# Two attention layers: the causal mask added on VectorE instead of TensorE, score units cut anew, the maxima's transfer put ahead of the keys', and the selection products of a slot in two parts

## The chip, the cores and the metric

The kernel runs on one core of a Trainium2 chip. The metric is the device time of one execution in microseconds. Five engines of the core matter: TensorE (PE in the profile, with PEld for its weight loads), VectorE (DVE), ScalarE (ACT), GpSimd (POOL) and SyncE (SP), which here only issues DMAs. Each works through its own list of instructions in order; they wait for each other by semaphores.

## The reference, cut to what matters

The program is two transformer-like layers over 16 sequences of 512 tokens with 128 channels. Each layer has one attention stage that this change touches. The first (called mla) projects to latents and has a rotary part; the second (mha) is plain:

```python
scores = jnp.einsum('bqhd,bkhd->bhqk', qq, kk) * scale      # 16 heads of 8
scores = jnp.where(causal[None, None], scores, jnp.finfo(scores.dtype).min)
probs = jax.nn.softmax(scores, axis=-1)
y = jnp.einsum('bhqk,bkhd->bqhd', probs, v).reshape(B, S, H)
```

What has to be computed for a head is: the scores of 512 queries with the keys up to each query, the maximum of each row, exp(score less maximum), the sum over keys, and the weighted values.

## The kernel before, in words

The stages run one after the other: a convolution layer's stages, attention mla, a layer of experts (glu), attention mha, and a second layer of experts (moe). Both attentions are made by one function, `attention_stage` (line 789).

**Turns and slots.** One sequence is a turn. A turn has four slots, g = 0 to 3, one for each group of four heads. `walk` (line 874) runs the first turn without probabilities, then a loop of inner turns, then turns without a next sequence, and a last one that only finishes. Each engine has its own function `slots` and walks over units k = 0, 1, 2, ... of a slot. What stands at which k is set by small tables (lines 863 to 872).

**Scores for the maxima.** TensorE computes scores of a unit (`scores`, L1394) into one of three PSUM banks, with queries on the partitions: 11 units for a slot (`UNITS1`). One matmul more for each unit (L1398) adds the mask: an identity times a table of 0 and -1e30. VectorE reduces each unit to its negated row maximum (L1101). After the last unit of a slot GpSimd splits the maxima into a high and a low part (L1187, L1188). In the next slot, behind unit k = 4, TensorE transposes them (L1441) and multiplies the previous output by selection matrices (L1446, four products of 128 by 36), VectorE copies the transposed maxima into `mhl` (L1068), and SyncE sends `mhl` by DMA into two extra rows of `Qb` (L952).

**Scores less maxima, probabilities, values.** One slot later TensorE recomputes the scores transposed, with the maxima as two more rows of the product (L1406): 10 units of 512 columns for a slot, 16 matmuls. ScalarE takes exp (L1297), GpSimd zeroes what lies above the diagonal (L1216), and in the slot after that TensorE multiplies by the values (L1414, four heads side by side in the array), in two places of a slot.

**The next sequence's queries and keys.** During a turn the projections for the next one are computed: latents in slot 0 (mla alone), keys and queries in slot 1, values in slot 2. They are split in high and low parts (`kh`, `kl`, `qh`, `ql`; the low parts by VectorE, L1059). SyncE copies them to the rows of `Kb` (three DMAs of 256 KB, L925 and L926) and `Qb` (twelve DMAs of 64 KB, each from 32 partitions to 8, L933 and L936). The keys' DMAs wait for `kb_used`, which TensorE gives at the end of slot 1. At the start of a turn TensorE waits for all fifteen (`k_rows`, `q_rows`) and for the maxima sent last (`m_rows`). SyncE's own list for an inner turn is: maxima in slot 0; maxima in slot 1; keys, maxima, queries in slot 2; maxima in slot 3.

## Time and profile before

| what | us |
|---|---|
| median of 3 runs (3221.18 to 3238.54) | 3233.5 |
| the profiled execution | 3232.98 |
| its span | 3231.2 |
| attention mla: first score unit reduced to last | 555.4 to 1347.4 |
| attention mha: first score unit reduced to last | 1903.1 to 2647.9 |

The profile is of one execution; its page gives the busy time of each engine, slices of the span, groups of instructions by line, waits and DMAs. "Busy" for TensorE is modelled (matmuls overlap, each row's duration holds the time through the array), so spacing between the starts of rows says more than their durations. A row of a timeline gives start, duration (both us), engine, line, operation, out<-in, sizes, how many instructions are merged, and in brackets the idle time before them and what ended it. PEclk is the granted TensorE clock as a share of 2.4 GHz. Over the whole span PE is busy 81%, DVE 67%, ACT 44%, POOL 36%. Both attentions together are about half of the time.

### The profile page before, as it was taken

To read this page: it belongs to the slowest core of one execution; us is meant where nothing else is said; L and a number is where in the kernel's file an instruction comes from. 1 tells how busy PE (TensorE), PEld (TensorE's weight loads), DVE (VectorE), ACT (ScalarE), POOL (GpSimd) and SP (SyncE) were. 2 spreads that over 40 slices of the span, in tenths; PEclk is the share of its full clock that TensorE was granted. 3 is DMA by queue.
4 is the path that set the end of the run, shared out by engine and by line. 5 is a ranking of instruction groups with operands and counts; after the bars stand their busy time and mean duration, and the time that the engine had idled before them with its cause. 6 is when DMAs were issued, how large, how long until landed. Compare 5 with 4: busy or idle time off the path is not lost. (4 is left out here: it accounts for less than half of the span.)

```text
span 3231.2 us, 51537 instructions
## 1 busy us (share of the span) xinstructions
PE 2618.4 (81%) x17479; PEld 2011.4 (62%) x17479; DVE 2178.6 (67%) x5628; ACT 1414.6 (44%) x2412; POOL 1177.9 (36%) x2298
## 2 busy tenths in 40 slices
PE   1445873999999999948888759999999997698972
PEld 1423662777777777636666647777777766486861
DVE  5733773777777767448888846676767754677785
ACT  0001330455555555511111225666666652586861
POOL 3210110334434344322222113454455442773076
PEclk9997995899999999969999969999999995799996
DMA  2144001213223222031110032222122114697772
GB/s 29 32 134 127 23 13 30 41 29 44 42 29 47 37 34 41 15 104 50 49 49 32 3 43 33 31 40 36 25 40 40 26 17 165 231 296 225 250 218 73
DMA packets 198657, 228.02 MB, mean 71 GB/s; under 512 B 48621, under 2 KB 148814, under 8 KB 190478
## 3 DMA queue, kind: packets, MB, share of 16 engines
q1 hardware_dynamic: 188302, 207.69, 26.7%
q0 software_dynamic: 8192, 16.79, 1.6%
q10 hardware_dynamic: 2048, 2.10, 0.2%
q8 instruction: 60, 0.98, 0.1%
q14 instruction: 55, 0.45, 0.0%
HBM read 132.55 MB, written 58.10 MB: 59 GB/s over the span
## 5 line engine op out<-in xcount | busy, mean ns | idle before, releaser
L1394 PE MATMUL banks<-Kb,Qb 96*128 96x128 f32 (+3 forms) x2048 | 599.6, 348 | 58.6 <-issue 27.3
L1406 PE MATMUL banks<-Qb,Kb 98*128 98x512 f32 (+3 forms) x2048 | 602.7, 356 | 4.8 <-ACT mha_prob L1297 1.0
L1101 DVE TENSOR_REDUCE mha_nm<-banks 128x1 f32<-128x384 f32 (+3 forms) x704 | 421.5, 639 | 185.9 <-PE banks L1398 172.3
L1101 DVE TENSOR_REDUCE mla_nm<-banks 128x1 f32<-128x384 f32 (+3 forms) x704 | 419.9, 638 | 160.0 <-PE banks L1398 146.5
L1297 ACT ACTIVATE mla_prob<-banks 128x512 f32<-128x512 f32 x640 | 376.5, 598 | 311.6 <-PE banks L1406 303.2
L1394 PEld LDWEIGHTS banks<-Kb,Qb 96*128 96x128 f32 x2048 | 364.3, 195 | 216.5 <-issue 159.9
L1297 ACT ACTIVATE mha_prob<-banks 128x512 f32<-128x512 f32 x640 | 375.7, 598 | 273.7 <-PE banks L1406 260.8
L1216 POOL TENSOR_SCALAR_AFFINE_SELECT mla_prob<-mla_prob 128x256 f32<-128x256 f32 (+1 forms) x640 | 237.8, 379 | 405.3 <-PE banks L1394 379.7
L1406 PEld LDWEIGHTS banks<-Qb,Kb 98*128 98x128 f32 x2048 | 334.8, 193 | 47.1 <-issue 7.6
L1216 POOL TENSOR_SCALAR_AFFINE_SELECT mha_prob<-mha_prob 128x256 f32<-128x256 f32 (+1 forms) x640 | 225.6, 361 | 355.4 <-PE banks L1394 329.2
L1828 PE MATMUL banks<-glu_wd,glu_hid 128*128 128x128 f32 x1024 | 147.7, 288 | 74.3 <-DVE glu_hid L1707 74.1
L1828 PEld LDWEIGHTS banks<-glu_wd,glu_hid 128*128 128x128 f32 x1024 | 130.5, 196 | 117.6 <-DVE glu_hid L1707 113.8
L2174 DVE TENSOR_TENSOR moe_hl<-moe_h,moe_hh 128x512 fp32r<-128x512 f32 x212 | 146.4, 692 | 78.7 <-ACT moe_h L2278 65.7
L1788 ACT ACTIVATE glu_sg<-banks 128x512 f32<-128x512 f32 x128 | 76.4, 597 | 262.2 <-PE banks L1802 262.2
L2277 ACT ACTIVATE moe_hh<-banks,moe_bt 128x512 fp32r<-128x512 f32 x212 | 146.1, 689 | 87.7 <-PE banks L2291 72.3
L1398 PE MATMUL banks<-mla_mask,mla_identr 128*128 128x128 f32 (+2 forms) x704 | 183.8, 261 | 0.0
L2227 POOL DMA_INDIRECT moe_gb<-results,moe_back_slot x128 | 131.2, 1025 | 143.5 <-SPq L1988 105.6
L1398 PE MATMUL banks<-mha_mask,mha_identr 128*128 128x128 f32 (+2 forms) x704 | 181.5, 258 | 0.0
L1414 PE MATMUL banks<-mla_prob,mla_V 128*9 128x512 f32 (+3 forms) x2048 | 169.1, 450 | 0.3
L1414 PE MATMUL banks<-mha_prob,mha_V 128*9 128x512 f32 (+3 forms) x2048 | 167.4, 446 | 0.2
L2214 POOL DMA_INDIRECT slots<-X,moe_slot x128 | 126.5, 988 | 67.3 <-issue 38.7
L1398 PEld LDWEIGHTS banks<-mla_mask,mla_identr 128*128 128x128 f32 x704 | 139.2, 198 | 8.5
(434 smaller groups left out, 5392.1 us busy)
## 6 DMA issues: line engine op xcount, KB each, us to landing
moe_wt<-expert_rows SPq DMA_DIRECT2D x53, 1024.0 KB
conv_tz<-conv_kernel SPq DMA_DIRECT2D x16, 1024.0 KB, 6.8
moe_xg<-slots SPq DMA_DIRECT2D x53, 256.0 KB
results<-moe_yt SPq DMA_DIRECT2D x53, 256.0 KB
Kb<-mla_kh SPq DMA_DIRECT2D x32, 256.0 KB, 4.9
Qb<-mla_qh SPq DMA_DIRECT2D x128, 64.0 KB
Kb<-mha_kh SPq DMA_DIRECT2D x32, 256.0 KB, 5.6
Qb<-mha_qh SPq DMA_DIRECT2D x128, 64.0 KB
```

What stands on the lines that cost most here:

```text
L1101: dve.tensor_reduce(nm[:, g % 2, h:h + heads, j], ps[:, bank1(g, k), 0:heads * w].rearrange("p (h k) -> p h k", h=heads), axis=AX.X, op=AL ...
L1216: pool.affine_select(out=part, in_=part, compare_op=ALU.is_ge, fill=0.0, base=0, pattern=pattern, channel_multiplier=-1).then_inc(p_ready, 1)
L1297: act.activation(prob[:, g % 2, k, :], ps[:, S2 + k % 2, :], ACT.Exp, scale=HD ** -0.5).then_inc(s2_free, 1)
L1394: one = pe.matmul(ps[:, bank, x * w:(x + 1) * w], Qb[0:MROW, u, g, h + x, j * P:(j + 1) * P], Kb[0:MROW, u, g, 0:w], start=(x == 0), stop= ...
L1398: pe.matmul(ps[:, bank, 0:heads * w].rearrange("p (x w) -> p x w", x=heads)[:, :, w - P:w], identr[:, :], mask[:, 0:heads, :], start=False ...
L1406: last = pe.matmul(ps[:, S2 + k % 2, at:at + w], Kb[0:MROW + 2, u, grp, kb * P:(kb + 1) * P], Qb[0:MROW + 2, u, grp, h, kb * P:L], start=T ...
L1414: last = pe.matmul(ps[32 * hh:32 * hh + HD + 1, OB, kb * P:L], V[:, u, kb, grp * HG + hh, :], prob[:, par, unit, at:at + w], start=(kb == ...
L1828: last = pe.matmul(ps[:, OB + e % 2, b * P:(b + 1) * P], hid[:, e % 2, b * P:(b + 1) * P], wd[:, e, :], start=True, stop=True)
L2174: dve.tensor_tensor(hl[:, k, :], h[:, k, :], f32(hh[:, k, :]), ALU.subtract).then_inc(hid_ready, 1)
L2214: pool.indirect_dma_start(slots_d, bass.IndirectOffsetOnAxis(slot[:, q, a, t:t + 1], 0), X[:, first + j, b, :], None).then_inc(scattered[q ...
L2227: pool.indirect_dma_start(gb[:, j % 2, a, b, :], None, res_d[q], bass.IndirectOffsetOnAxis(back_slot[:, q, a, t:t + 1], 0)).then_inc(gathe ...
L2277: act.activation(hh[:, k, :], ps[:, FB + k, :], ACT.Gelu_apprx_tanh, bias=bias)
```

## The change

- **Mask.** The mask matmuls are gone. VectorE's reduction of a piece is now `tensor_tensor_reduce`: it reads the scores and a mask table in SBUF, adds, negates, takes the minimum, and writes the sum to a scrap tile `junk`; it compiles to two instructions, the main one and one that writes the result.
- **Units.** A slot has 12 score units for the maxima: four of one piece of 512, four of a piece of 384 and one of 128, four of one piece of 256 (`ROWS`). It has 11 units of scores less maxima, 11 matmuls: four of 512, four of 384, and three of 512 in which two or four heads share one matmul (`UNITS2`). The values follow in three places (k = 5, 8, 10), each waiting for its own units.
- **Selection.** The transposed maxima and the first two selection products come behind k = 2, the other two behind k = 3.
- **Low parts and the rotary sum** move from VectorE to GpSimd (`low_part`, `add_turned`), and get tiles of their own (`sines`, `tmpq`).
- **Places.** The output product moves from slot 1 to slot 0; mla's keys are at (1,0) and (1,6), its queries at (1,9) and (1,11); mha's queries move to slot 2; the values' projection moves to slot 3.
- **SyncE.** In slot 2 the maxima's DMA comes ahead of the keys and the queries; the queries' pieces go in another order.

```diff
-UNITS1 = [(0, 0, HG)] + [(1, h, 2) for h in (0, 2)] + [(j, h, 1) for j in (2, 3) for h in range(HG)]
+UNITS = 3 * HG
+ROWS = [[(3, 0, L)], [(2, 0, 3 * P), (0, 3 * P, P)], [(1, 0, 2 * P)]]
+UNITS2 = [(0, h, 1) for h in range(HG)] + [(1, h, 1) for h in range(HG)] + [(2, 0, 2), (2, 2, 2), (3, 0, 4)]
...
-        KEYS = dict(pe=0, turn=2, act=5, low=6) if latent else dict(pe=0, act=2, low=4)
-        QUERIES = dict(pe=6, turn=8, act=10, low=1) if latent else dict(pe=6, act=8, low=9)
-        VALUES = dict(pe=7, act=9)
-        DENSE = dict(pe=WIDE, act=WIDE, pe2=WIDE, dve=WIDE, add=(6, 8), stats=6)
+        GATHER, VALUES_AT, OUT, SPLIT = 2, {5: (0,), 8: (1,), 10: (2, 3)}, 11, 9
+        DENSE = dict(pe=(0, 3), dve=(0, 5), add=((0, 8), (0, 10)), stats=(0, 7))
+            KEYS = dict(pe=((1, 0), (1, 6)), turn=(1, 7), add=(1, 8), act=(1, 10), low=(2, 0))
+            QUERIES = dict(pe=((1, 9), (1, 11)), turn=(2, 0), add=(2, 2), act=(2, 3), low=(2, 5))
+            NEXT_XS = dict(stats=(2, 8), rms=(2, 11), scale=((3, 1), (3, 3)))
+            KEYS = dict(pe=((1, 0),), act=(1, 2), low=(1, 4))
+            QUERIES = dict(pe=((2, 1),), act=(2, 3), low=(2, 5))
+        VALUES = dict(pe=(3, 1), act=(3, 3))
...
                 def slots(n, u, turn, prep, proj, dense):
                     for g in range(NG):
+                        if has_maxima(turn, g):
+
+                            par, grp, to = (g + 1) % 2, (g + 3) % NG, u if g else 1 - u
+                            sp.wait_ge(ml_ready, c.next(ml_ready))
+                            sp.dma_start(f32(Qb[MROW:MROW + 2, to, grp, :, :]),
+                                         f32(mhl[:, par, :])).then_inc(m_rows[par], 16)
                         if g == 2 and turn != "last":
                             sp.wait_ge(kb_used, c.next(kb_used))
                             if proj:
                                 keys(1 - u)
-                        if has_maxima(turn, g):
-
-                            par, grp, to = (g + 1) % 2, (g + 3) % NG, u if g else 1 - u
-                            sp.wait_ge(ml_ready, c.next(ml_ready))
-                            sp.dma_start(f32(Qb[MROW:MROW + 2, to, grp, :, :]),
-                                         f32(mhl[:, par, :])).then_inc(m_rows[par], 16)
-                        if g == 2 and turn != "last" and proj:
-                            queries(1 - u)
+                                queries(1 - u)
...
+                def row_maxima(g, k):
+                    h = k % HG
+                    dve.wait_ge(s1_ready, c.next(s1_ready))
+                    for j, at, w in ROWS[k // HG]:
+                        last = dve.tensor_tensor_reduce(junk[:, k % 3, at:at + w], ps[:, bank1(k), at:at + w], mask[:, L - w:L], -1.0,
+                                                        BIG, ALU.add, ALU.min, nm[:, g % 2, h, j:j + 1])
+                    last.then_inc(s1_free, 1)
...
+                def add_turned(parts, full, whole, product):
+                    pool.wait_ge(parts, c.next(parts))
+                    pool.tensor_tensor(whole[:, :], whole[:, :], product[:, :], ALU.add).then_inc(full, 1)
+
+                def low_part(high, whole, hi, lo, split_done):
+                    pool.wait_ge(high, c.next(high))
+                    pool.tensor_tensor(lo[:, :], whole[:, :], f32(hi[:, :]), ALU.subtract).then_inc(split_done, 1)
...
-                    pe.matmul(ps[:, bank, 0:heads * w].rearrange("p (x w) -> p x w", x=heads)[:, :, w - P:w],
-                              identr[:, :], mask[:, 0:heads, :], start=False, stop=True,
-                              skip_group_check=True).then_inc(s1_ready, 1)
+                def scores(g, u, k):
+
+                    h = k % HG
+                    pe.wait_ge(s1_free, c.next(s1_free))
+                    for j, at, w in ROWS[k // HG]:
+                        last = pe.matmul(ps[:, bank1(k), at:at + w], Qb[0:MROW, u, g, h, j * P:(j + 1) * P],
+                                         Kb[0:MROW, u, g, 0:w], start=True, stop=True)
+                    last.then_inc(s1_ready, 1)
```

Three places of the lists of instructions follow, each before and then after the change. The first is TensorE in the later units of a slot of mla (L1394 and L1411 are scores for the maxima, L1406 and L1420 scores less maxima, L1398 the mask, L1414 and L1427 the values).

```order
L1394 MATMUL banks<-Kb,Qb 128x512
L1398 MATMUL banks<-mla_mask,mla_identr 128x128
L1406 MATMUL banks<-Qb,Kb 128x512
L1394 MATMUL banks<-Kb,Qb 128x512
L1398 MATMUL banks<-mla_mask,mla_identr 128x128
L1406 MATMUL banks<-Qb,Kb 128x128
L1406 MATMUL banks<-Qb,Kb 128x384
L1414 MATMUL banks<-mla_prob,mla_V 9x256 x4
```

```order
L1411 MATMUL banks<-Kb,Qb 128x384
L1411 MATMUL banks<-Kb,Qb 128x128
L1420 MATMUL banks<-Qb,Kb 128x384
L1411 MATMUL banks<-Kb,Qb 128x256
L1420 MATMUL banks<-Qb,Kb 128x512
L1427 MATMUL banks<-mla_prob,mla_V 9x384 x4
```

The mask matmul behind each unit is gone, and the narrow piece of 128 columns has moved from the scores less maxima to the scores for the maxima. The second place is SyncE from the maxima of slot 1 on in an inner turn of mla (`mla_mhl` are the maxima, `mla_kh` and `mla_kl` the keys, `mla_qh` and `mla_ql` the queries; "waits" names the semaphore).

```order
L925 DMA Kb<-mla_kh 32x4x512 [waits mla_k_split,mla_kb_used]
L925 DMA Kb<-mla_kh 32x4x512
L926 DMA Kb<-mla_kl 32x4x512
L952 DMA Qb<-mla_mhl 2x16x128 [waits mla_ml_ready]
L933 DMA Qb<-mla_qh 8x4x512 [waits mla_q_split]
L933 DMA Qb<-mla_qh 8x4x512 x7
L936 DMA Qb<-mla_ql 8x4x512 x4
L952 DMA Qb<-mla_mhl 2x16x128 [waits mla_ml_ready]
```

```order
L954 DMA Qb<-mla_mhl 2x16x128 [waits mla_ml_ready] x4
L935 DMA Kb<-mla_kh 32x4x512 [waits mla_k_split,mla_kb_used]
L935 DMA Kb<-mla_kl 32x4x512
L935 DMA Kb<-mla_kh 32x4x512
L942 DMA Qb<-mla_qh 8x4x512 [waits mla_q_split]
L942 DMA Qb<-mla_qh 8x4x512
L942 DMA Qb<-mla_ql 8x4x512
L942 DMA Qb<-mla_qh 8x4x512 x2
```

The maxima of slot 2 now stand ahead of the keys; nothing stands between keys and queries any more, and the maxima of slot 3 still stand behind the queries. The third place is VectorE in mla, around the rotary step of the keys in slot 1 (`sinr` and `cosr` are the tables of sines and cosines).

```order
L1101 TENSOR_REDUCE mla_nm<-banks 128x2 x2
L1052 TENSOR_TENSOR mla_xs<-banks,mla_sinr 128x512
L1053 TENSOR_TENSOR mla_tmp<-banks,mla_cosr 128x512
L1055 TENSOR_TENSOR mla_tmp<-mla_tmp,mla_xs 128x512
L1101 TENSOR_REDUCE mla_nm<-banks 128x1 x2
L1068 CAST mla_mhl<-banks 32x128
```

```order
L1093 ISA mla_junk,mla_nm<-banks,mla_mask 128x384
L1093 ISA mla_nm 128x1
L1093 ISA mla_junk,mla_nm<-banks,mla_mask 128x128
L1093 ISA mla_nm 128x1
L1056 TENSOR_TENSOR mla_sines<-banks,mla_sinr 128x512
L1057 TENSOR_TENSOR mla_tmp<-banks,mla_cosr 128x512
L1093 ISA mla_junk,mla_nm<-banks,mla_mask 128x256
```

One reduction of up to four heads has become a pair of instructions for every head and piece: 16 pairs for a slot where 11 reductions stood; and the sum of the two products (L1055) has left VectorE.

## Rows read from the trace of the kernel before

**Rows 1.** Busy time by stretch: a steady stretch of mla, one of mha.
```profile
core 0: us, PE busy (x) PEld busy (x) DVE busy (x) ACT busy (x) POOL busy (x), PEclk, DMA share, GB/s
800.00:1000.00 200.00, 194.53 (x1495) 146.05 (x1494) 154.42 (x315) 116.27 (x206) 85.54 (x223) 1.00 0.25 38
...
2200.00:2400.00 200.00, 196.52 (x1561) 149.90 (x1551) 140.04 (x287) 123.78 (x216) 97.34 (x249) 1.00 0.25 37
```
**Rows 2.** Timeline of TensorE: the first unit of slots and turns.
```profile
849.00 0.63 PE L1394 MATMUL banks<-Kb,Qb 96*128 96x128 f32 x4 [0.79 <-DVE mla_nm L1101]
...
875.36 0.63 PE L1394 MATMUL banks<-Kb,Qb 96*128 96x128 f32 x4 [0.29 <-issue]
...
948.26 0.64 PE L1394 MATMUL banks<-Kb,Qb 96*128 96x128 f32 x4 [0.79 <-DVE mla_nm L1101]
...
1987.80 0.63 PE L1394 MATMUL banks<-Kb,Qb 96*128 96x128 f32 x4 [0.37 <-DVE mha_nm L1101]
...
2011.75 0.63 PE L1394 MATMUL banks<-Kb,Qb 96*128 96x128 f32 x4 [0.26 <-DVE mha_nm L1101]
...
2130.07 0.63 PE L1394 MATMUL banks<-Kb,Qb 96*128 96x128 f32 x4 [0.30 <-DVE mha_nm L1101]
```
**Rows 3.** Timeline of TensorE, single units of mla.
```profile
856.55 0.22 PE L1398 MATMUL banks<-mla_mask,mla_identr 128*128 128x128 f32 x1
856.61 0.50 PE L1406 MATMUL banks<-Qb,Kb 98*128 98x128 f32 x2
856.95 0.40 PE L1339 MATMUL banks<-mla_xth,mla_lath 128*96 128x512 f32 x1
857.18 0.40 PE L1340 MATMUL banks<-mla_xth,mla_latl 128*96 128x512 f32 x1
```
**Rows 4.** Timeline of VectorE, mla.
```profile
850.66 2.81 DVE L1101 TENSOR_REDUCE mla_nm<-banks 128x4 f32<-128x512 f32 x5 [1.71 <-PE banks L1398]
...
883.05 0.38 DVE L108 BATCH_NORM_AGGREGATE mla_mv<-mla_st 128x2 f32<-128x6 f32 x4
...
883.83 0.16 DVE L1036 TENSOR_TENSOR mla_var<-mla_var,mla_mv 128x4 f32<-128x4 f32 x1
```
**Rows 5.** Timeline of SyncE: a turn of mha, then the same places in mla.
```profile
2011.57 1.24 SPq L925 DMA_DIRECT2D Kb<-mha_kh  x2
...
2016.81 0.66 SPq L952 DMA_DIRECT2D Qb<-mha_mhl  x1
2017.52 6.86 SPq L933 DMA_DIRECT2D Qb<-mha_qh  x8
...
881.78 0.67 SPq L952 DMA_DIRECT2D Qb<-mla_mhl  x1
```
**Rows 6.** Stretches of the same turn of mha: DMA share and GB/s.
```profile
2014.00:2018.40 4.40, 4.40 (x37) 2.91 (x36) 2.95 (x8) 1.92 (x4) 4.12 (x7) 1.00 1.03 122
...
2025.00:2031.20 6.20, 6.20 (x51) 4.49 (x49) 4.36 (x10) 3.55 (x8) 2.58 (x7) 1.00 0.52 62
2031.20:2032.20 1.00, 1.00 (x8) 0.88 (x7) 0.93 (x3) 1.00 (x2) 0.63 (x2) 1.00 0.12 11
```
**Rows 7.** mha's second turn starts: TensorE's row, then stretches around it.
```profile
1938.82 0.63 PE L1394 MATMUL banks<-Kb,Qb 96*128 96x128 f32 x4 [1.52 <-DMA Qb<-mha_mhl]
...
1937.70:1938.80 1.10, 0.00 (x0) 0.01 (x1) 0.34 (x1) 0.42 (x1) 0.42 (x2) 1.00 0.00 0
...
1940.90:1947.70 6.80, 6.80 (x35) 4.39 (x33) 2.66 (x7) 2.14 (x4) 1.01 (x3) 0.50 0.01 2
```
**Rows 8.** Stretches of the convolution stage, then of mla.
```profile
205.90:210.40 4.50, 0.13 (x8) 0.12 (x8) 0.69 (x1) 0.00 (x0) 0.40 (x1) 1.00 0.99 276
210.40:213.80 3.40, 3.40 (x24) 1.04 (x25) 0.00 (x0) 0.00 (x0) 0.00 (x0) 0.50 0.75 287
...
1122.00:1125.20 3.20, 2.39 (x14) 1.67 (x14) 3.05 (x6) 2.00 (x4) 1.34 (x3) 0.99 0.34 76
1125.20:1128.50 3.30, 3.30 (x14) 3.20 (x14) 3.02 (x6) 1.44 (x4) 2.53 (x6) 0.50 1.07 128
```

More of the change, by code:

```diff
@@ L943, in slots @@
                     for g in range(NG):
-                        if g == 2 and turn != "last":
-                            sp.wait_ge(kb_used, c.next(kb_used))
-                            if proj:
-                                keys(1 - u)
                         if has_maxima(turn, g):
@@ L1335, in _, with three @@
                 pe.sem_inc(s2_free, 2)
-                def three(o, hi, lo, a, first=True, last=True):
+                def three(o, hi, lo, first=True, last=True):
                     pe.matmul(o, hi, xth[:, :], start=first, stop=False)
@@ new lines, in new_values @@
+                def new_values():
+                    pe.wait_ge(ma_free, c.next(ma_free))
+                    for b in range(BLK):
+                        tok = slice(b * P, (b + 1) * P)
+                        o = ps[:, MA, tok]
+                        if latent:
+                            last = pe.matmul(o, lats[:, 1, tok], up[:, 3, :], start=True, stop=True)
+                        else:
+                            pe.matmul(o, xth[:, tok], wph[:, 1, :], start=True, stop=False)
+                            pe.matmul(o, xth[:, tok], wpl[:, 1, :], start=False, stop=False)
+                            last = pe.matmul(o, xtl[:, tok], wph[:, 1, :], start=False, stop=True)
+                    last.then_inc(v_ready, 1)
@@ L1502, in _ @@
                 pe.drain().then_inc(xs_taken, 1)
-                for g in range(NG):
-                    project(g, 0)
+                if latent:
+                    latents(1)
+                    latents(0)
+                for part in range(len(KEYS["pe"])):
+                    keys(part)
+                for part in range(len(QUERIES["pe"])):
+                    queries(part)
+                new_values()
                 transpose_x()
```

383 lines of the change are left out of this document (178 added, 205 removed).

## The prediction

> **What bounds the kernel now.** I read the busy times by stretch first. In both attentions TensorE is busy 97 to 98% of the time at the full granted clock (194.5 and 196.5 of 200 us), VectorE 77% and 70%, ScalarE about 60%, GpSimd 43% and 49% [rows 1]. So TensorE sets the pace inside a turn. Then the timeline of TensorE, for the rhythm: mla takes 99.26 us for two turns (849.00 to 948.26), 49.6 for one, of which slots 0 and 1 take 26.36; mha takes 142.27 for three (1987.80 to 2130.07), 47.4 for one, of which slots 0 and 1 take 23.95 [rows 2]. Last the timeline of SyncE and the stretches with DMA traffic, because TensorE may not start a turn before the keys, the queries and slot 3's maxima have landed. There the reader is to see a second chain that is only just hidden, as long as about half a turn. I think that this chain decides.
>
> **The chain of transfers.** In a turn of mha the first keys' DMA is issued at 2011.57 [rows 5]. From 2014 to 2018.4 the keys move at 122 GB/s with all DMA engines busy; then the queries move at 62 GB/s with half of them busy, with no pause, until the last maxima at about 2032 [rows 6]. That is 20.4 us from the first keys' issue to the last maxima, and in this turn keys and queries are back to back, as they will be after the change. From data there to TensorE going on it is another 1.2 us: in mha's second turn nothing moves from 1937.70 on, and TensorE starts at 1938.82, after 1.52 us of waiting for exactly this DMA [rows 7]. So a turn can't start earlier than 21.6 us after its keys' issue. Before, the keys are issued when slot 1 ends, which is why it fits in slots 2 and 3 (23.3 and 23.5 us, rows 2).
>
> **What the change does to TensorE.** Gone are 11 mask matmuls for a slot, 2048 columns. A 512 column matmul takes 0.23 us (856.95 to 857.18), a narrow mask matmul 0.06 (856.55 to 856.61), and a narrow one makes its neighbour late: 128 and 384 columns take 0.34 together [rows 3], 0.11 more than one of 512, which I put half on each. Masks: 2048 columns at 0.23 us for 512 is 0.92, and nine narrow ones at 0.05 is 0.45, so 1.37. Fewer, wider units of scores less maxima: four splits less, -0.2. A third break for the values and a second for the selection: +0.3, taken as three breaks at the 0.11 of the split; it lies between 0 and 0.5. Net -1.3 us for a slot, with 0.9 to 1.6 as its ends. Slots 0 and 1 of mla then take 26.36 - 2.6 = 23.8. In mha the queries leave slot 1 as well (three matmuls of 512, 0.7): 23.95 - 2.6 - 0.7 = 20.6. TensorE alone would need 49.6 - 5.2 = 44.4 for a turn of mla and 42.2 for one of mha.
>
> **VectorE.** Five reductions, three of 512 and two of 384, took 2.81 us [rows 4]: about 0.60 and 0.465 from start to start, so 0.33 for 256 and 0.20 for 128 columns. Before: 7 x 0.60 + 4 x 0.465 = 6.06 a slot. After: four heads x (0.60 + 0.465 + 0.33 + 0.20) = 6.38, plus 16 instructions that write a result. The trace has none of these. From below: four small aggregations in 0.38 us, 0.07 for each further one. From above: 0.16, the duration of a tiny operation, plus the 0.08 by which a reduction's duration (0.68) exceeds its spacing, if the second waits for the first: 0.24 [rows 4]. I take 0.07, since nothing between the two instructions waits on a semaphore: 16 x 0.07 = 1.1, so 7.5 a slot, +1.4. Four operations of 512 (0.6 to 0.9 us) leave for GpSimd in a turn of mla, two in mha: -0.75 and -0.4 a slot. VectorE goes from 9.6 to 10.2 us a slot in mla and from 8.3 to 9.3 in mha: below TensorE's 11.1 and 10.6, but in mla's slot 2, which gets the queries' rotary step beside the statistics, VectorE needs 11.4. GpSimd gets these operations; even at 2 us each they add 8 us to the 21 it is busy in a turn of mla. ScalarE gets one unit more a slot. Both are covered.
>
> The Trainium skill (VectorE: DVE Perf Modes, section "Two Vector instructions with no wait between them") says that an operation which also writes its accumulator is two instructions, each held back only by different start quadrants. All operands here start at partition 0. By that rule 0.07 is right; the trace of before can't show it.
>
> **What the change does to the chain.** The maxima of slot 2 now go first on SyncE, so the keys' DMA waits for them. They are issued 5.1 us after TensorE starts slot 2 in mha (2011.75 and 2016.81) and 6.4 us in mla (875.36 and 881.78) [rows 2, 5]. After: VectorE needs 4 x 0.67 + 0.8 = 3.5 us for units 0 to 4 instead of 2.7, in mla 1.2 more for the rotary step, but it comes into slot 2 less late, TensorE having more to spare of it: I take 4.9 us in mha and 5.9 in mla. One issue takes 0.7 (2016.81 to 2017.52). The new turn's start after the start of slot 2 is then
> - mla: 5.9 + 0.7 + 20.4 + 1.2 = 28.2 us, where slots 2 and 3 need about 22;
> - mha: 4.9 + 0.7 + 20.4 + 1.2 = 27.2 us, where they need 21.7.
>
> The queries' split isn't late for this: it stands behind unit 5 of 12, so about 6 us into slot 2, and takes GpSimd 2 us at most, while the keys occupy the queue for 6.7 us from their issue (2011.57 to 2018.3), until 12 us into the slot. So TensorE stands still for about 6 us at the end of each turn. Turn: mla 23.8 + 28.2 = 52.0, mha 20.6 + 27.2 = 47.8. Added work and the lost cover together eat all of what the masks give.
>
> **The clock.** 4.4 us of idle TensorE (205.9 to 210.4) was followed by 3.4 us at half the clock, 1.2 GHz, with TensorE busy; in mla a stretch with only 2.39 of 3.2 us busy was followed by half the clock too [rows 8], and the 1.5 us wait at 1938 by 6.8 us of it [rows 7]. After 6 us of idle I expect it at each turn's start, where TensorE is the bound: 3.4 us at half speed loses 1.7 us, 6.8 would lose 3.4. I take 1.7. Turn: mla 53.7, mha 49.5.
>
> **Sum.** 14 turns of each attention: 14 x (53.7 - 49.65) + 14 x (49.5 - 47.4) = 57 + 29 = 86. Before already has two stretches of 10 us at half clock in mla (one of them in rows 8), 9 us that are not lost twice: -9. First turns, which have no probabilities and so are short in slots 0 and 1: mha's grows from 37 to about 44 since the chain is as long there, mla's by 2: +9. Last turns have nothing to fetch: 4 x -1.3 each, -10. Sum +76. The profiled execution took 3232.98 us, 1.8 more than its span and within 0.02% of the median of 3233.5, so the sum stands for both: 3233 + 76 = 3309 us. The ends: 1.6 instead of 1.3 a slot and no clock loss, 3245; 0.9 and 3.4 us of clock loss, 3385.
>
> **Rivals.**
> - *The clock holds.* As above without the 1.7: 14 x (2.35 + 0.4) = 38, and +9 - 10, so 3270 with the 9 us kept. For it: a turn has one long pause only, and mla's turns mostly kept the clock.
> - *The result write is dear* (0.24). 16 x 0.17 = 2.7 us more VectorE a slot: 12.9 in mla, above TensorE in slots 0 and 1 by about 1 each, and 1 later at slot 2's maxima: some +3 in mla, +4 in mha with the finishing statistics in slot 0. 14 x 7 = 98: 3407. Against it: the small aggregations overlap.
> - *Faster: the queries spread over more DMA engines.* They move with a DMA share of 0.52 [rows 6]. The new order alternates rows of three parts of `Qb`. If the bound is the rows written to, they could go at the pace of issue, 0.71 us from start to start (2016.81 to 2017.52, rows 5): twelve take 8.5 us instead of the 12.8 from 2018.4 to 2031.2, the chain is 4.3 shorter: mla 49.4, mha 45.2 with the clock's loss. 14 x -2.45 = -34, less the 9 and 1: 3189. It decides once the chain of 20.4 is under 18. Against it: the last four DMAs of a turn already go to changing rows and gain nothing, the rate being 62 GB/s throughout [rows 6].
> - *Faster: the chain doesn't bind*, the slots do: mla 23.8 + 22 = 45.8, mha 42.2. 14 x -9.05 = -127, -18 for the rest (the 9 of the clock, and the first and last turns): about 3088. For it speaks only that I may misjudge when the keys can go; the list of SyncE says that they can't.
>
> The Trainium skill (DMA: Bandwidth & Descriptors, section "Why a DMA increments its semaphore by 16 and not by 1") says that a DMA from SyncE runs on as many engines, up to 16, as divide the slowest dimension on both sides: 8 for 32 partitions to 8. The share of 0.52 agrees; by that rule the order of the pieces changes nothing, and the third rival falls.
>
> **Chances.** Forecast 0.42; clock holds 0.15; dear write 0.10; spread queries 0.14; chain not binding 0.11; the last 0.08 for sums that cancel within the bound. No change, within 0.5% (16 us, about what a measurement of this kernel can tell): 0.10, of it 0.02 from the second case. Slower by more 0.65, faster by more 0.25. The likeliest case's own range is 3245 to 3385. The range reaches into the faster cases as far as the spread queries, and leaves out the unbound chain and the dearest write: 3175 to 3385.
>
> **What would show it.** On TensorE's first unit of a turn a wait of 4 to 7 us for the DMA of the maxima, turns 52 to 54 and 47.5 to 50 us long; keys issued 5.5 to 7 us into slot 2; half clock in the first microseconds of a turn; the pair on VectorE at 0.67 us for 512 columns. Wrong if turns start with no wait for a DMA, or if the keys' DMAs stand at the end of slot 1.

## The result, and the profile after

The changed kernel takes 3360.2 us (median of 4, 3348.7 to 3370.1) where the kernel before takes 3234.4: a ratio of 1.0395, 95% interval 1.0349 to 1.0441, 126 us more. The forecast was 76 more, 3309, in a range of 3175 to 3385. The profiled execution's span is 3347.0 us against 3231.2, 116 more; the two attention stages, from first to last instruction on their tiles, hold 114 of it: mla 953 us for 894, mha 895 for 839. One of run 8's four executions below took 4206.9 us, at a mean granted clock of 0.57 where the other three had 0.87, and is in no comparison.

First the waits of TensorE, whole kernel (line, what it waited for, us in total, times, longest):

```profile
PE banks L1411 <- DMA Qb<-mla_mhl: 72.8, 14, 5.8
PE banks L1411 <- DMA Qb<-mha_mhl: 70.7, 14, 5.5
```

There are 28 waits for the maxima's DMA, 5.1 us each: one at the start of every turn from the third on. The second turn, behind the short first one, waits 1.5 us in mla and 0.9 in mha. In the kernel before there is one such wait [rows 7]. Then the timeline around one turn of mla and one of mha, TensorE's rows:

```profile
813.56 0.76 PE L1411 MATMUL banks<-Kb,Qb 96*128 96x512 f32 x1 [5.78 <-DMA Qb<-mla_mhl]
...
842.03 0.47 PE L1411 MATMUL banks<-Kb,Qb 96*128 96x512 f32 x1 [0.26 <-DVE mla_nm L1093]
...
868.79 0.77 PE L1411 MATMUL banks<-Kb,Qb 96*128 96x512 f32 x1 [5.26 <-DMA Qb<-mla_mhl]
...
2286.93 0.47 PE L1411 MATMUL banks<-Kb,Qb 96*128 96x512 f32 x1 [0.26 <-issue]
...
2313.48 0.76 PE L1411 MATMUL banks<-Kb,Qb 96*128 96x512 f32 x1 [5.35 <-DMA Qb<-mha_mhl]
```

and SyncE's:

```profile
847.56 0.64 SPq L954 DMA_DIRECT2D Qb<-mla_mhl  x1
848.31 0.60 SPq L935 DMA_DIRECT2D Kb<-mla_kh  x1
...
2292.72 0.59 SPq L935 DMA_DIRECT2D Kb<-mha_kh  x1
```

Slot 2 of mla starts at 842.03, its maxima go at 847.56, the keys behind them at 848.31, and TensorE starts the next turn at 868.79: 20.5 us after the keys' issue, 26.8 after the start of slot 2, where slots 2 and 3 took 23.3 [rows 2]. In mha the same stretch is 5.8 + 20.8 = 26.6 us. A turn of mla takes 55.2 us (813.56 to 868.79), of mha 52.2 on average over 13 turns. Last the stretches, with the granted clock as the third number from the end:

```profile
700.00:1250.00 550.00, 484.64 (x3070) 317.59 (x3070) 373.44 (x1580) 288.40 (x550) 258.49 (x630) 0.90 0.24 35
800.00:1000.00 200.00, 173.45 (x1079) 115.08 (x1078) 129.18 (x545) 100.87 (x194) 88.63 (x220) 0.87 0.23 33
2200.00:2400.00 200.00, 174.48 (x1149) 117.58 (x1152) 127.22 (x569) 110.28 (x208) 95.31 (x241) 0.90 0.22 29
...
842.03:863.40 21.37, 20.55 (x144) 12.78 (x144) 18.13 (x81) 14.15 (x29) 15.01 (x34) 1.00 0.49 64
863.50:868.70 5.20, 0.03 (x1) 0.00 (x0) 0.43 (x2) 0.38 (x1) 0.00 (x0) 0.86 0.37 47
867.30:880.80 13.50, 12.01 (x44) 8.94 (x45) 5.50 (x20) 3.75 (x7) 3.14 (x10) 0.50 0.01 3
```

TensorE's busy share has gone from 97 and 98% [rows 1] to 87%. A mean granted clock of 0.90 over ten turns of mla is a fifth of the time at half clock, 11 us of each turn. In the turn shown it stands still from 863.5 to 868.7; the granted clock is 0.50 (1.2 GHz) from 867.3 to 880.8, so TensorE works for 12 us at that level. The half clock begins inside the wait and outlasts it.

### The profile page after: what moved, and what is told of

Its sections match the earlier page's. It is cut to its first block and busy times, and to the rows that moved or that the text cites. A ratio compares the mean times of both kernels' runs of the same rounds, so it can differ in the third digit from the quotient of the medians.

```text
span 3347.0 us, 51624 instructions
## 1 busy us (share of the span) xinstructions
PE 2583.1 (77%) x15431; PEld 1847.6 (55%) x15431; DVE 2170.4 (65%) x8218; ACT 1415.1 (42%) x2540; POOL 1298.6 (39%) x2522
## 3 DMA queue, kind: packets, MB, share of 16 engines
q1 hardware_dynamic: 188302, 207.69, 26.8%
## 5 line engine op out<-in xcount | busy, mean ns | idle before, releaser
L1411 PE MATMUL banks<-Kb,Qb 96*128 96x512 f32 (+3 forms) x2048 | 669.7, 375 | 183.9 <-DMA Qb<-mla_mhl 72.8
L1093 DVE CUSTOM_DVE_ANT_0 mha_junk<-banks,mha_mask 128x512 bf16<-128x512 f32 (+3 forms) x1024 | 462.1, 488 | 294.2 <-PE banks L1411 286.3
L1411 PEld LDWEIGHTS banks<-Kb,Qb 96*128 96x128 f32 x2048 | 395.2, 208 | 435.9 <-issue 219.4
L1093 DVE CUSTOM_DVE_ANT_0 mla_junk<-banks,mla_mask 128x512 bf16<-128x512 f32 (+3 forms) x1024 | 457.2, 488 | 271.1 <-PE banks L1411 254.0
L1420 PE MATMUL banks<-Qb,Kb 98*128 98x512 f32 (+1 forms) x1408 | 599.9, 432 | 22.4 <-ACT mha_prob L1312 11.1
L1312 ACT ACTIVATE mla_prob<-banks 128x512 f32<-128x512 f32 (+1 forms) x704 | 378.4, 558 | 372.3 <-PE banks L1420 371.5
L1312 ACT ACTIVATE mha_prob<-banks 128x512 f32<-128x512 f32 (+1 forms) x704 | 375.0, 558 | 354.8 <-PE banks L1420 350.9
L1214 POOL TENSOR_SCALAR_AFFINE_SELECT mla_prob<-mla_prob 128x128 f32<-128x128 f32 (+2 forms) x704 | 238.1, 347 | 420.9 <-PEq L1419 414.6
L1214 POOL TENSOR_SCALAR_AFFINE_SELECT mha_prob<-mha_prob 128x128 f32<-128x128 f32 (+2 forms) x704 | 236.8, 346 | 406.3 <-PEq L1419 395.8
L1420 PEld LDWEIGHTS banks<-Qb,Kb 98*128 98x128 f32 x1408 | 289.3, 206 | 83.0 <-issue 68.2
L1427 PE MATMUL banks<-mla_prob,mla_V 128*9 128x512 f32 (+3 forms) x2048 | 182.4, 453 | 0.0
L1427 PE MATMUL banks<-mha_prob,mha_V 128*9 128x512 f32 (+3 forms) x2048 | 177.0, 442 | 0.0
L2294 ACT ACTIVATE moe_h<-banks,moe_bt 128x512 f32<-128x512 f32 x212 | 144.5, 681 | 0.0
L1704 DVE SCALAR_TENSOR_TENSOR glu_acc<-banks,glu_wts,glu_acc 128x128 f32<-128x128 f32 x448 | 125.4, 342 | 0.2 <-PE banks L1844 0.2
```

Of the source, the lines that this page charges most:

```text
L1093: last = dve.tensor_tensor_reduce(junk[:, k % 3, at:at + w], ps[:, bank1(k), at:at + w], mask[:, L - w:L], -1.0, BIG, ALU.add, ALU.min, nm ...
L1214: pool.affine_select(out=part, in_=part, compare_op=ALU.is_ge, fill=0.0, base=0, pattern=[[0, n], [1, P]] if n > 1 else [[1, P]], channel_ ...
L1312: act.activation(prob[:, g % 2, START[k]:START[k] + w], ps[:, bank2(g, k), 0:w], ACT.Exp, scale=HD ** -0.5).then_inc(s2_free, 1)
L1411: last = pe.matmul(ps[:, bank1(k), at:at + w], Qb[0:MROW, u, g, h, j * P:(j + 1) * P], Kb[0:MROW, u, g, 0:w], start=True, stop=True)
L1420: pe.matmul(ps[:, bank2(g, k), 0:WIDE[k]].rearrange("p (x w) -> p x w", x=heads), Kb[0:MROW + 2, u, grp, kb * P:(kb + 1) * P], Qb[0:MROW + ...
L1427: last = pe.matmul(ps[32 * hh:32 * hh + HD + 1, OB, kb * P:L], V[:, u, kb, grp * HG + hh, :], prob[:, par, at:at + L - kb * P], start=(kb ...
```

## The experiments

All comparisons are with the kernel before on the same chip. Runs 1 to 4 and 8 to 10 ran on chips where the last stage of experts, which no run touches, takes 672 to 682 us, not 533 to 535, so the kernel before takes 3368 to 3376 there and a ratio is a little nearer to 1. The two columns on the right, the attention stages in each kernel's trace, don't have this.

| kernel | ratio to before, 95% interval | mla us | mha us |
|---|---|---|---|
| before | 1 | 894 | 839 |
| changed | 1.0395 (1.0349 to 1.0441) | 953 | 895 |
| 1 keys first | 1.0122 (1.0087 to 1.0158) | 903 | 863 |
| 2 before, maxima first | 1.0692 (1.0661 to 1.0723) | 1021 | 949 |
| 3 busy wait | 1.0112 (1.0070 to 1.0153) | 908 | 855 |
| 4 keys first and earlier | 1.0103 (1.0068 to 1.0138) | 913 | 860 |
| 5 changed, again | 1.0386 (1.0368 to 1.0403) | 947 | 899 |
| 6 places moved | 1.0153 (1.0136 to 1.0170) | 968 | 808 |
| 7 before, mask on VectorE | 1.0194 (1.0177 to 1.0211) | 929 | 859 |
| 8 ready in time | 1.0151 (1.0120 to 1.0182) | 968 | 811 |
| 9 values last | 1.0134 (1.0100 to 1.0167) | 968 | 818 |
| 10 as 8, mask on TensorE | 1.0571 (1.0523 to 1.0619) | 1062 | 885 |
| 11 as 7, and useless work | 1.0299 (1.0272 to 1.0326) | 956 | 869 |
| 12 mla of before, mha of 6 | 0.9898 (0.9875 to 0.9922) | 893 | 803 |

**1. The keys first again.**

```diff
                     for g in range(NG):
+                        if g == 2 and turn != "last":
+                            sp.wait_ge(kb_used, c.next(kb_used))
+                            if proj:
+                                keys(1 - u)
                         if has_maxima(turn, g):
...
-                                keys(1 - u)
-                                queries(1 - u)
+                        if g == 2 and turn != "last" and proj:
+                            queries(1 - u)
```

> The changed kernel with one thing undone: on SyncE's list of slot 2 the keys' transfers stand first again, then the maxima, then the queries. Theory A (the order of the list is what costs; the keys' issue starts a chain of 20.3 to 21.0 us that ends in TensorE's wait): in mha the keys go at the end of slot 1, the chain ends about 21 us into slots 2 and 3, which take 20.9, and a turn falls from 52.2 to 43.5-44.5 us; in mla the keys' low part is ready only 3.1 us into slot 2 and the queries' 8.3 us into it, the chain ends at 23.8 us against the slots' 21.4, and a turn falls from 55.2 to 48.5-51. In all about 3165 us (3135 to 3185), the waits for the maxima's DMA in mha gone. Theory B (the waits come from slower transfers or from the mask on VectorE, not from the order): no more than 20 us are gained, 3340 to 3360.

The order alone gives 50 us in mla and 32 in mha, 82 of the 114, where theory A wanted 195 and B at most 20. A is right on what costs and too simple on what is left: it also had mha's waits gone, and 14 are left, 3.0 us each, with turns of 49.9 us on average in mha and 52.1 in mla. In mha, SyncE and GpSimd show the second wait (the last line is a stretch with its DMA share and GB/s at the end):

```profile
2220.05 0.59 SPq L935 DMA_DIRECT2D Kb<-mha_kh  x1
...
2225.30 0.66 SPq L958 DMA_DIRECT2D Qb<-mha_mhl  x1
2229.99 1.45 SPq L942 DMA_DIRECT2D Qb<-mha_qh  x2
```

```profile
2223.31 3.13 POOL L1202 TENSOR_SCALAR mha_xm<-mha_xm,mha_mv,mha_rstd 128x128 f32<-128x128 f32 x4
...
2228.68 1.29 POOL L1186 TENSOR_TENSOR mha_ql<-mha_tmpq,mha_qh 128x512 fp32r<-128x512 f32 x1
...
2228.00:2230.00 2.00, 2.00 (x28) 0.94 (x20) 1.02 (x6) 1.29 (x3) 2.00 (x5) 1.00 0.00 0
```

The queries' low part stands on GpSimd behind the normalisation (L1202) and comes ten us into slot 2, some 3 us after the keys have moved: from 2228 to 2230 nothing moves. In mla the keys wait for their own split, until 3.1 us into slot 2 (835.50, slot 2 starts at 832.36), and go with the maxima right behind them in the queue; slot 3 then waits for those, and here 1.6 us of standing still were followed by 10 us at half the clock:

```profile
844.57 0.64 PE L1412 MATMUL banks<-Kb,Qb 96*128 96x512 f32 x1 [1.59 <-DMA Qb<-mla_mhl]
```

```profile
844.90:855.00 10.10, 10.10 (x37) 7.11 (x37) 4.91 (x19) 3.86 (x7) 6.22 (x15) 0.50 0.40 63
```

**2. The order alone, in the kernel before.** The reverse of the edit of run 1, in the kernel before.

> The kernel before, with only SyncE's list changed as the change does it: in slot 2 the maxima, then the keys, then the queries. Theory A (the order alone starts the chain late): mla's keys go 7.1 us into slot 2, a turn is 26.3 + 7.1 + 20.6 = 54.0 us and with 3.9 for the clock 57.9; mha's go 5.8 us into it, 23.8 + 5.8 + 20.6 = 50.2, with the clock 54.1; 3233 + 14 x 8.2 + 14 x 6.6 - 9 = about 3430 us (3390 to 3450), more than the whole change costs. Theory B (the order is harmless by itself): 3225 to 3245.

232 us slower, nearly twice what the whole change costs. B falls. Theory A is right in kind and 35 us short: it wanted 197 more, 217 at most. SyncE's row and TensorE's:

```profile
817.48 1.25 SPq L925 DMA_DIRECT2D Kb<-mla_kh  x2
```

```profile
838.40 0.45 PE L1393 MATMUL banks<-Kb,Qb 96*128 96x128 f32 x1 [5.25 <-DMA Qb<-mla_mhl]
```

With the queries' pieces in their old order, the chain from the keys' issue to the turn's start takes 20.9 us; with the new order 20.5 to 20.8. The order of the pieces makes a few tenths at most.

**3. TensorE busy while it waits.**

```diff
+                        held = g == 0 and turn == "inner" and dense
+                        if held:
+                            pe.wait_ge(s1_free, c.next(s1_free))
+                            for _ in range(20 if latent else 28):
...
                         if g == 0 and turn != "last":
                             pe.wait_ge(k_rows, c.next(k_rows, 3 * 16))
```

> The changed kernel with TensorE busy during the wait at a turn's start: 20 matmuls of 512 columns (mla) or 28 of 384 (mha), about 4.6 us at full clock, whose result is overwritten, before it waits for the transfers. Theory A (the idle 5 us are what brings the half clock of some 10 us behind them, at 0.41 us lost for each us at half clock): the granted clock stays 1.0, turns are 51.6 us in mla and 48.8 in mha, 3360 - 85 = about 3275 us (3255 to 3290). Theory B (the half clock comes from something else, such as the load of the unit that follows): the clock stays low behind each turn's start, and the time is 3350 to 3375.

The matmuls put in multiply constants into the bank of unit 0, which overwrites them. By their stages the two attentions take 44 and 40 us less than in the changed kernel's trace, 84 where 85 were expected, and the clock holds:

```profile
812.24 0.47 PE L1412 MATMUL banks<-Kb,Qb 96*128 96x512 f32 x1 [0.90 <-DMA Qb<-mla_mhl]
...
836.71 0.47 PE L1412 MATMUL banks<-Kb,Qb 96*128 96x512 f32 x1 [0.26 <-DVE mla_nm L1093]
```

```profile
800.00:1000.00 200.00, 190.01 (x1249) 122.03 (x1249) 141.49 (x597) 108.96 (x209) 97.16 (x240) 0.99 0.24 34
2200.00:2400.00 200.00, 190.82 (x1345) 133.50 (x1346) 134.38 (x602) 116.70 (x221) 102.30 (x260) 1.00 0.26 34
```

Work of no use makes the changed kernel faster. This kernel also gives the slots at full clock: slots 0 and 1 of mla take 24.5 us (812.24 to 836.71) where they took 26.36 [rows 2].

**4. The keys' steps one place earlier.** In the table, `KEYS = dict(pe=((1, 0), (1, 5)), turn=(1, 6), add=(1, 7), act=(1, 9), low=(1, 10))`, beside run 1's order.

> As the run with the keys first, and in mla the keys' later steps one place earlier (second product (1,5) for (1,6), rotary step (1,6) for (1,7), sum (1,7) for (1,8), high part (1,9) for (1,10), low part (1,10) for (2,0)). Theory A (the chain of transfers bounds mla's turn from the keys' split): the keys go up to 2.5 us earlier, but the queries' split at 8.3 us into slot 2 then takes their place, so a turn is 0.5 to 1.5 us shorter than with the keys first alone, 7 to 20 us in all; mha is unchanged. Theory B (mla's turn is bound by TensorE once the keys go first): no difference, within 3 us.

No difference that can be measured from run 1 (3414.4 and 3412.7 us); mla's stage is 10 us longer in the trace, not shorter. Theory B's number, but not for its reason: TensorE still waits for the maxima's DMA, 14 times and 19.6 us in mla. The keys now go 2.9 us into slot 2, for 3.1 in run 1: the step one place earlier gains 0.2 us, not 2.5.

**5. The changed kernel again.** 

> The changed kernel unchanged, as the reference for the other kernels on the chip that they run on. Attention mla takes 952 us and mha 895 us in its first trace; both theories expect the same again, within 10 us each.

A ratio of 1.0386, mla 947 and mha 899: as before, within 6 us.

**6. Places moved.** Run 1's order, and

```diff
-            KEYS = dict(pe=((1, 0), (1, 6)), turn=(1, 7), add=(1, 8), act=(1, 10), low=(2, 0))
-            QUERIES = dict(pe=((1, 9), (1, 11)), turn=(2, 0), add=(2, 2), act=(2, 3), low=(2, 5))
+            KEYS = dict(pe=((1, 0), (1, 5)), turn=(1, 6), add=(1, 7), act=(1, 8), low=(1, 9))
+            QUERIES = dict(pe=((1, 7), (1, 8)), turn=(1, 9), add=(1, 10), act=(1, 11), low=(2, 1))
...
-            QUERIES = dict(pe=((2, 1),), act=(2, 3), low=(2, 5))
+            QUERIES = dict(pe=((1, 5),), act=(1, 7), low=(1, 9))
```

> The changed kernel with the keys first on SyncE and its places moved so that what the transfers wait for is ready in time: mla's keys at (1,5) with low part (1,9), its queries at (1,7) and (1,8) with low part (2,1), mha's queries back in slot 1 with low part (1,9), ahead of GpSimd's normalisation. Theory A (keys first alone left two waits, the maxima behind the late keys in mla, 1.6 us, and in mha the queries' split 10 us into slot 2; both bring half the clock with them): without them a turn is what TensorE's slots need, 46.3 us in mla and 43.7 in mha; mla takes about 827 us and mha 777, some 245 less than the changed kernel and 115 less than the kernel before. Theory B (the added units and three places for the values cost TensorE more than the masks gave, and the slots bind): turns stay above 49 and 47 us, no faster than the kernel before.

Half of A's gain in mha, B for mla. In mha no wait for a DMA is left, two turns take 92.3 us (2343.32 to 2435.59), 46.1 for one where two took 95.0 before (2082.80 to 2177.82), 47.5 for one; the stage takes 808 us, 31 less than the kernel before (A wanted 62), 87 less than the changed one. In mla the steps are too close behind each other: ScalarE waits for GpSimd's sum with the exponentials queued behind it.

```profile
PE banks L1421 <- ACT mla_prob L1313: 60.3, 19, 4.3
...
ACT mla_qh L1284 <- POOL mla_tmpq L1182: 64.2, 16, 5.4
```

The turns of mha, on TensorE's timeline:

```profile
2343.32 0.47 PE L1412 MATMUL banks<-Kb,Qb 96*128 96x512 f32 x1 [1.45 <-DVE mha_nm L1094]
...
2435.59 0.47 PE L1412 MATMUL banks<-Kb,Qb 96*128 96x512 f32 x1 [1.46 <-DVE mha_nm L1094]
```

**7. The mask alone, in the kernel before.**

```diff
-                    pe.matmul(ps[:, bank, 0:heads * w].rearrange("p (x w) -> p x w", x=heads)[:, :, w - P:w],
-                              identr[:, :], mask[:, 0:heads, :], start=False, stop=True, ...
...
-                                dve.tensor_reduce(nm[:, g % 2, h:h + heads, j], ...
+                                for x in range(heads):
+                                    last = dve.tensor_tensor_reduce(junk[:, k % 3, x * w:(x + 1) * w], ...
```

> The kernel before with the mask alone changed: no mask matmuls, VectorE adds the mask in 16 reductions for a slot where 11 stood; units, places and SyncE's list as before. Theory A (masks cost TensorE 1.37 us a slot): slots 0 and 1 take 23.6 us in mla and 21.2 in mha, then the chain of transfers, 21.2 to 21.6 us, is 0.6 to 1 us longer than slots 2 and 3: turns of 45.0 and 42.6 us, 3233 - 14 x 4.65 - 14 x 4.85 - 9 = about 3092, 140 us less than the kernel before (110 to 155). Theory B (the short wait for the transfers that this uncovers brings half the clock, at 4 us a turn): 30 to 60 us less. Theory C (VectorE with 16 operations becomes the bound): no gain.

61 us slower. None of the three fits: A and B wanted a gain, C no change. First two stretches of the kernel before, 550 us of mla and 500 of mha:

```profile
700.00:1250.00 550.00, 535.47 (x4046) 400.84 (x4047) 418.60 (x853) 314.23 (x556) 230.87 (x599) 0.98 0.25 38
2050.00:2550.00 500.00, 491.66 (x3899) 375.77 (x3896) 349.94 (x720) 308.75 (x539) 241.37 (x626) 1.00 0.24 36
```

Then the same stretches of run 7, the 20 us around one fall of its clock, and its waits:

```profile
700.00:1250.00 550.00, 504.60 (x3378) 341.44 (x3380) 411.48 (x1663) 288.14 (x524) 207.84 (x564) 0.90 0.23 35
2050.00:2550.00 500.00, 477.23 (x3291) 324.66 (x3291) 349.88 (x1544) 288.01 (x518) 229.30 (x599) 0.91 0.24 34
929.30:939.50 10.20, 8.83 (x70) 5.56 (x69) 8.90 (x25) 4.71 (x10) 2.70 (x7) 1.00 0.20 51
939.60:949.70 10.10, 10.10 (x43) 7.15 (x44) 7.46 (x39) 3.18 (x6) 5.57 (x12) 0.50 0.54 75
```

```profile
PE banks L1399 <- DVE mla_nm L1102: 48.0, 54, 2.6
PE banks L1399 <- DVE mha_nm L1102: 22.2, 44, 1.3
```

TensorE had 8.83 of 10.20 us busy, with one wait of 1.08 us on VectorE, and then worked 10 us at half the clock. The waits themselves are 41 us more than before (17.3 and 12.1 there), and the granted clock is 0.90 and 0.91 against 0.98 and 1.00. What that costs can be read where the clock stays at full for four slots in a row. In mha, the starts of a slot 2, of the next turn and of its slot 2:

```profile
2138.94 0.41 PE L1399 MATMUL banks<-Kb,Qb 96*128 96x128 f32 x2 [0.26 <-issue]
...
2162.09 0.41 PE L1399 MATMUL banks<-Kb,Qb 96*128 96x128 f32 x2 [0.42 <-DVE mha_nm L1102]
...
2184.25 0.41 PE L1399 MATMUL banks<-Kb,Qb 96*128 96x128 f32 x2 [0.26 <-issue]
```

These four slots take 45.3 us, and four in mla 48.1 (995.90 to 1043.97), less than the 47.5 and 49.6 of the kernel before. The mean turns are 49.1 and 53.2. So without the masks TensorE is faster at full clock, and stretches at half clock take more than that back.

**8. Ready in time.** As run 6 for mha. In mla the rotary sum is VectorE's again, `KEYS = dict(pe=((1, 0), (1, 5)), turn=(1, 6), act=(1, 8), low=(1, 10))`, `QUERIES = dict(pe=((1, 7), (1, 9)), turn=(1, 10), act=(2, 1), low=(2, 3))`.

> As the run with the moved places for mha (where mha took 808 us). In mla ScalarE had waited there for GpSimd's sum and held up the exponentials (60 us of TensorE's waits); here the rotary sum is VectorE's again, right behind the two products, keys at (1,5), rotary step (1,6), high part (1,8), low part (1,10), queries at (1,7) and (1,9), rotary step (1,10), high part (2,1), low part (2,3). Theory A (transfers that start in time and no held-up exponentials leave TensorE's slots, 46.3 us a turn): mla 835 to 860 us, 35 to 60 less than the kernel before; in all some 3150 us, 80 less than the kernel before. Theory B (wherever TensorE isn't full, the half clock takes the gain back): mla 885 us or more, in all no more than 30 less.

mla 968 us again: B's number. ScalarE no longer holds TensorE up (1.8 us of waits for 60.3), but not everything is ready in time: GpSimd finishes the keys' low part 3.9 us into slot 2 (850.53 to 854.4), the maxima stand behind the keys again, and slot 3 waits for them.

```profile
863.55 0.50 PE L1404 MATMUL banks<-Kb,Qb 96*128 96x512 f32 x1 [2.72 <-DMA Qb<-mla_mhl]
...
700.00:1250.00 550.00, 500.64 (x2962) 327.62 (x2965) 373.42 (x1535) 279.67 (x529) 226.31 (x585) 0.84 0.21 33
```

The granted clock over those 550 us of mla is 0.84, the kernel before has 0.98 there.

**9. The last values behind unit 11.** Otherwise run 8; `VALUES_AT` is `{5: (0,), 8: (1,), 11: (2, 3)}`.

> As the run before it, with the last values (key blocks 2 and 3) behind unit 11 of a slot rather than unit 10. At every second turn's start TensorE stood 1.45 us (0.79 in the kernel before) where the loop goes round, and 3.4 us of half clock followed. Theory A (the loop's way back is hidden by the matmuls still queued, and the last unit is too short for it): the gap goes to 0.8 us or less and its half clock is gone, 7 x 1.4 us in each attention, some 15 to 20 us less in all. Theory B (the gap doesn't depend on what stands before it, and ScalarE gets the output later): 0 to 20 us more.

3420.2 for 3425.2 us, not to be told apart; mha's stage 7 us longer, and the gaps where the loop goes round are 1.76 and 0.84 us in mha, not 1.46 and 0.1. Theory A falls.

**10. As run 8, the mask on TensorE.** A narrow matmul behind each piece, plain reductions on VectorE, as in the kernel before.

> As the run with the transfers ready in time, with the mask back on TensorE (16 narrow matmuls a slot, one for each piece) and plain reductions on VectorE. Theory A (mask matmuls cost 2048 columns, 0.92 us, and 16 x 0.05): 1.7 us more a slot on TensorE, 6.9 a turn, 28 turns: 150 to 190 us more than that run. Theory B (the busier TensorE keeps its clock, which pays for part of it): 60 to 120 us more, the granted clock 1.0 all through both attentions.

146 us more by the medians; by the stages 93 in mla and 74 in mha, in a profiled execution that was its longest (3587.4 us, median 3570.9). Nearer to A, 1.2 us a slot in mha (74 us over 15 turns of four slots), and the busier TensorE doesn't keep its clock, which B wanted: the granted clock is 0.95 in mha (2050 to 2550) and in mla 0.82, with TensorE 95% busy:

```profile
700.00:1250.00 550.00, 523.07 (x3251) 375.48 (x3250) 335.97 (x840) 258.92 (x482) 212.09 (x537) 0.82 0.20 31
```

In this arrangement of units the mask on VectorE is worth its place.

**11. As run 7, with useless work on TensorE.**

```diff
+                    if k in (8, 9, 10):
+                        pe.matmul(ps[:, bank, 0:w], Qb[0:MROW, u, g, h, j * P:(j + 1) * P],
+                                  Kb[0:MROW, u, g, 0:w], start=True, stop=True)
```

> The kernel before with the mask on VectorE (that run took 929 us for mla and 859 for mha, 61 us more in all than the kernel before, and its granted clock fell behind waits of 0.3 to 1.2 us on VectorE), and with useless work put in on TensorE: in each slot the scores of units 8, 9 and 10 are computed twice (3 x 512 columns, 0.7 us a slot, the first result overwritten), where the masks had taken 1.37. Theory A (the loss is the clock's: TensorE just short of full loses half its clock for 3 to 14 us at a time, and a fuller TensorE keeps it): the clock stays at 1.0 for most of both attentions, turns are 49.65 - 5.5 + 2.8 = 47.0 us in mla and 44.8 in mha, bounded by the slots, and the kernel is 40 to 75 us faster than the kernel before although 78 us of work are put in. Theory B (VectorE's reductions bound the kernel with the mask on VectorE, and the clock only follows): the extra work lies beside VectorE's at no gain, 30 to 80 us slower than the kernel before. Theory C (TensorE bound, the clock indifferent to it): 61 + 78, some 140 us slower.

96 us slower than the kernel before, 35 more than run 7. The clock does go up where work was put in:

```profile
700.00:1250.00 550.00, 511.06 (x3365) 348.76 (x3365) 399.86 (x1615) 281.15 (x507) 202.69 (x548) 0.91 0.23 35
2050.00:2550.00 500.00, 482.62 (x3397) 332.49 (x3395) 349.85 (x1529) 290.04 (x514) 226.87 (x594) 0.96 0.23 33
```

```profile
PE banks L1402 <- DVE mla_nm L1102: 41.1, 62, 3.4
```

but in mla hardly, where the waits on VectorE stay, and nowhere does it pay for the work. Theory A falls as a recipe: what helped in run 3 was work inside the wait; work beside it is only more work. More of it than half of what the masks had taken wasn't tried. B's range is the nearest, and just missed.

**12. The better half of each.** mla with the function of the kernel before, mha with run 6's.

> A kernel made of both: attention mla as in the kernel before, attention mha as in the run with the moved places (the change with the keys first on SyncE and mha's keys and queries split in slot 1). If the two stages don't touch each other, mla takes 894 us again and mha 808 where it took 839: 31 us less than the kernel before, a ratio of 0.990 (0.987 to 0.993). If mha's gain belonged to the chip or to the state in which mla leaves the clock, no difference.

3191.9 us for 3228.0, a ratio of 0.9898 (0.9875 to 0.9922) where 0.990 was expected; mla 893 and mha 803 us in the trace. It is the fastest kernel of this study, 1% faster than the kernel before and by the two ratios some 5% faster than the changed one. Its mha keeps the clock with TensorE 94% busy:

```profile
2050.00:2550.00 500.00, 468.39 (x3317) 309.00 (x3315) 362.81 (x1629) 317.16 (x596) 275.69 (x708) 0.99 0.25 37
```

## Why the prediction came out right

**The mechanism** is the one forecast: the keys' issue moves behind slot 2's maxima, the chain behind it no longer fits, TensorE waits for slot 3's maxima at each turn's start. Run 2 shows it with nothing else changed, run 1 takes it back. Term by term:

| term | forecast mla, mha | measured mla, mha |
|---|---|---|
| start of slot 2 to the keys' issue | 6.6, 5.6 | 6.3, 5.8 |
| keys' issue to the turn's start | 21.6, 21.6 | 20.5, 20.4 |
| slots 0 and 1, full clock (run 3) | 23.8, 20.6 | 24.5, 22.4 |
| clock's loss | 1.7, 1.7 | about 3.9, 3.6 |
| turn | 53.7, 49.5 | 55.2, 52.2 |

The measured values are means over the 13 turns from the third on (646.33 to 1364.09 and 2050.80 to 2729.49 in the changed kernel's trace); the clock's loss is the turn less the other three. 14 x 1.5 + 14 x 2.7 = 59 us, against 51 between 3309 and 3360. Part of the closeness is luck: a chain 1.1 and 1.2 us too long in the forecast and slots 0 and 1 that are 0.7 and 1.8 us too short come to -32 and +35 us over 14 turns of each, and cancel. Of the signs that the prediction named, the wait, the keys' issue and the half clock at a turn's start came true; the turns lie above the 54 and 50 us that it gave as their upper ends.

**What was mis-sized: the clock.** The prediction took 3.4 us at half the clock behind each wait, from the one pause in the convolution stage [rows 8], and gave the 6.8 us behind the 1.5 us wait [rows 7] only as an end of the range. In the changed kernel it is 11 us in a mean turn of mla, and run 3 prices it: 84 us in all, 3 us a turn. The nearest rows, in the attentions themselves, were the dearer ones.

**And what the masks give.** 1.3 us a slot was forecast, 0.9 as the low end. In mla run 3 shows (26.36 - 24.47) / 2 = 0.95. In mha slots 0 and 1 take 22.46 us (2156.07 to 2178.53 in run 3's trace) for 23.95, of which 0.7 is the queries' leaving: 0.4 a slot, below the low end. Run 7 has the mask's share alone, at full clock: slots 0 and 1 take 22.16 us in mha (2162.09 to 2184.25) and 24.71 in mla (1019.26 to 1043.97), 0.9 and 0.8 a slot less than before, where the prediction put 1.37 (it counts nine narrow masks; there are eight, 0.05 us less). The rest of the change, put at +0.1 a slot, gives 0.1 in mla and costs 0.5 in mha. Of that 1.0 us in the two slots, 0.55 is one wait for ScalarE's exponentials (at 2172.31 in run 3); which part of the rest is splits and breaks wasn't tried. In slots 2 and 3 of mha the 1.3 does appear once the chain is out of the way: 20.7 us in run 6 (from 2461.05) where they took 23.3.

**VectorE.** The pair of instructions that takes the mask and writes the result follows at the pace of the plain reduction:

```profile
845.35 0.69 DVE L1093 CUSTOM_DVE_ANT_0 mla_junk<-banks,mla_mask 128x512 bf16<-128x512 f32 x1
845.96 0.08 DVE L1093 DVE_READ_ACCUMULATOR2_ANT mla_nm<- 128x1 f32 x1
845.96 0.69 DVE L1093 CUSTOM_DVE_ANT_0 mla_junk<-banks,mla_mask 128x512 bf16<-128x512 f32 x1
846.57 0.08 DVE L1093 DVE_READ_ACCUMULATOR2_ANT mla_nm<- 128x1 f32 x1
```

0.61 us from start to start for 512 columns, where 0.60 was the plain one and 0.67 the forecast: the write of the result costs 0.01, not 0.07, and the rival with 0.24 falls. The Trainium skill (VectorE: DVE Perf Modes, section "Two Vector instructions with no wait between them") has such an operation as two instructions that are held back only by other start quadrants (a quadrant is 32 partitions). This row agrees.

**The other rivals.** *The clock holds*: it didn't; run 3 shows its price, 3360 - 84 = 3276, and the prediction had worked out 3270 for it. *Queries spread over more engines*: the chain is 20.9 us with the old order of pieces (run 2) and 20.5 to 20.8 with the new, not 4.3 shorter. By the Trainium skill (DMA: Bandwidth & Descriptors, section "Why a DMA increments its semaphore by 16 and not by 1") the number of engines goes by the shape of a transfer, which is the same in both; the two runs agree. *The chain doesn't bind*: 28 waits say it does. But its number, 3088, was a promise that the freed time of TensorE can be had, and here the runs correct the prediction's picture most. With the chain out of the way run 6 gains 31 us in mha; in mla it loses 74; with the mask alone moved, run 7 loses 61. What the masks leave free on TensorE is idle time in small pieces, and the clock takes more than they gave. The prediction saw the half clock only behind waits of the chain.

**That queries' split isn't late** was right for the changed kernel, where it comes before the keys have moved (2296.72, and the keys were issued at 2292.72), and is what limits run 1: in a chain, the link that is hidden by the first one shows once the first is gone.

**Open:** why mla stays above 900 us in every arrangement tried but its old one (runs 1 to 11). The granted clock from 700 to 1250 us is 0.82 to 0.91 in runs 1, 4 and 6 to 11, so the half clock has a large part in it; what brings it on each time is not shown. Part is seen: the keys' split late on GpSimd and the maxima behind them (runs 1, 4, 8), ScalarE held up (run 6), VectorE behind (run 7). No run has all three gone. The selection products in two parts and the low parts on GpSimd were not tried by themselves.

## What to carry to other kernels

Before a transfer is put ahead of another on a queue, count from the one that is pushed back to the engine that needs it last: here 20.5 us of keys, queries and maxima fitted into two slots with some 3 us to spare (23.3 us of slots 2 and 3, and 0.2 before them), and 6 to 7 us of delay cost 232 us by themselves. Price work taken from a full TensorE with the half clock that its new idle time can bring: run 7 took off 0.8 to 0.9 us a slot and lost 61 us. The mean busy share doesn't tell which way it goes: at 94 to 95% busy the granted clock was 0.99 in run 12's mha and 0.82 in run 10's mla. And when two stages share one function, look at each alone: run 6's form of the change gained 31 us in one attention and lost 74 in the other, and the total hid the gain.
